# Attention and routed feed-forward block on one core: normalisation, transposition and router logits moved out of the front stage into the first units of the stream

## What is computed

```python
xn = _layernorm(x, axis=-1)
# attention: 16 heads of 64, causal
q, k, v = (einsum('btd,hdk->bhtk', xn, W) for W in (Wq, Wk, Wv))
wei = softmax(where(causal, q @ k.T * 64 ** -0.5, -inf))
attn = (wei @ v).reshape(...) @ Wo + bo
# feed-forward: a shared expert and the best 2 of 16 experts a token
router = sigmoid(xn @ gate_w + gate_b)           # 256 x 16
values, indices = top_k(router, 2); values = values / sum(values)
mlp = lambda x, wg, wu, wd: (silu(x @ wg) * (x @ wu)) @ wd
out = x + attn + xn + mlp(xn, shared) + sum(values * mlp(xn, experts[indices]))
```

## Time and profile before

| | us |
|---|---|
| median of 3 runs | 1964.02 (1962.02 to 1964.59) |
| the profiled execution | 1970.11 |
| its span in the trace | 1968.4 |
| front stage, to the stream's first transfer | 95.6 |
| unit 0 of the stream begins | 117.0 |
| the last `weigh` begins | 1956.3 |

### The profile page before, as it was taken

The page is one execution under the profiler, slowest core; times in us unless marked ns, Lnnn a source line. Parts: engine busy times, 40 slices in busy tenths (PEclk is TensorE's granted clock), DMA queues, the critical chain, the costliest instruction groups (busy, mean ns, idle before and its releaser), DMA issues.

```text
span 1968.4 us, 53517 instructions
## 1 busy us (share of the span) xinstructions
PE 1905.5 (97%) x20558; PEld 1751.7 (89%) x20558; DVE 1406.9 (71%) x4086; ACT 1208.4 (61%) x3340; POOL 1019.5 (52%) x1512
## 2 busy tenths in 40 slices
PE   6889999999999998999999999999999999999998
PEld 6878898988888898999998999999999989888897
DVE  7568886767676675666666667666667888888865
ACT  4356566666666665666665666666666666656564
POOL 2243447777777643344343343344444767687742
PEclk9999999999999999999999999999999999999999
DMA  9524422434343312545545445445422232323200
GB/s 260 187 106 176 161 77 85 143 110 136 109 145 109 126 51 83 181 162 163 166 148 170 155 152 168 161 161 183 146 92 76 87 119 87 117 89 119 76 23 12
DMA packets 158603, 249.92 MB, mean 127 GB/s; under 512 B 27280, under 2 KB 112528, under 8 KB 158352
## 3 DMA queue, kind: packets, MB, share of 16 engines
q1 hardware_dynamic: 134688, 150.79, 23.5%
q0 software_dynamic: 23664, 95.70, 15.0%
HBM read 151.54 MB, written 94.90 MB: 125 GB/s over the span
## 4 chain that ended last, share of the span: by engine, by line
PE 73%; POOL 12%; issue 7%; ACT 2%; DVE 1%; DMA 0%; POOLq 0%; SPq 0%; DVEq 0%
PE d_bank L658 15%; PE d_bank L710 11%; PE d_bank L696 10%; PE d_bank L685 9%; PE d_bank L671 7%; POOL d_probs L1305 7%; PE d_bank L726 7%; PE d_bank L784 6%; POOL queued_rows L1268 4%; PE d_bank L771 3%; PE d_bank L742 2%; ACT d_probs L853 2%; PE d_bank L794 1%; PE d_bank L731 1%; POOL d_base L1257 1%
## 5 line engine op out<-in xcount | busy, mean ns | idle before, releaser
L1305 POOL TENSOR_SCALAR d_probs<-d_probs,d_inverse 128x512 f32<-128x512 f32 (+3 forms) x1024 | 553.6, 556 | 767.4 <-DVE d_inverse L985 765.6
L853 ACT ACTIVATE d_probs<-d_probs,d_bias 128x512 f32<-128x512 f32 (+3 forms) x1024 | 561.1, 553 | 1.2 <-DVE d_bias L979 1.2
L979 DVE CUSTOM_DVE_ANT_0 d_probs<-d_bank,mask 128x512 f32<-128x512 f32 (+3 forms) x1024 | 438.9, 484 | 2.1 <-PE d_bank L696 1.9
L658 PE MATMUL d_bank<-d_xnt,wqk_all 128*128 128x512 f32 x1536 | 417.6, 408 | 1.5 <-DVE d_xnt L1032 1.5
L696 PE MATMUL d_bank<-d_ks,d_qs 64*128 64x512 f32 (+3 forms) x3072 | 317.4, 335 | 14.0 <-issue 12.0
L658 PEld LDWEIGHTS d_bank<-d_xnt,wqk_all 128*128 128x128 f32 x1536 | 276.6, 192 | 55.7 <-DVE d_xnt L1032 1.7
L846 ACT ACTIVATE d_probs_t<-d_bank 128x512 f32<-128x512 f32 (+1 forms) x384 | 188.8, 526 | 213.6 <-PE d_bank L685 213.5
L710 PE MATMUL d_bank<-d_probs_t,d_v 128*64 128x128 f32 x5120 | 308.6, 276 | 0.0
L710 PEld LDWEIGHTS d_bank<-d_probs_t,d_v 128*64 128x64 f32 x5120 | 277.7, 137 | 17.2 <-issue 5.4
L696 PEld LDWEIGHTS d_bank<-d_ks,d_qs 64*128 64x128 f32 x3072 | 252.0, 188 | 35.6 <-issue 19.4
L685 PEld LDWEIGHTS d_bank<-ident_r,d_probs_moved 64*128 64x128 f32 x5120 | 232.8, 136 | 38.6 <-issue 36.9
(11 more groups left out here) (122 smaller groups left out, 2296.9 us busy)
## 6 DMA issues: line engine op xcount, KB each, us to landing
queued_rows<-d_zeros SPq DMA_DIRECT2D x79, 256.0 KB, 2.4
d_x<-queued_rows SPq DMA_DIRECT2D x79, 256.0 KB, 3.4
routed_rows<-d_y SPq DMA_DIRECT2D x79, 256.0 KB, 2.3
expert_rows<-d_w SPq DMA_DIRECT2D x32, 384.0 KB, 3.8
a_x_in<-in_L_attn_x SPq DMA_DIRECT2D x16, 512.0 KB, 7.1
xn_rows<-a_xn SPq DMA_DIRECT2D x16, 512.0 KB, 5.2
d_normal<-xn_rows SPq DMA_DIRECT2D x32, 256.0 KB
d_base<-in_L_attn_x SPq DMA_DIRECT2D x32, 256.0 KB, 3.0
```

Source lines behind the costliest of these rows:

```text
L658: last = pe.matmul(to[:, :], wqk[:, n % PAIRS, "qk".index(kind), wa, k, :], xnt[n // PAIRS % 2][:, xb, k, :], start=first, stop=(k == KD - ...
L853: act.activation(part, part, ACT.Exp, bias=bias[:, i, h:h + 1], scale=-1.0, accum_out=total[which][:, at % 4:at % 4 + 1]).then_inc(exp_don ...
L979: dve.tensor_tensor_reduce(out=probs[:, i, h, 0:cols], in0=bank(f"s{fill}", u, h)[:, at * P:at * P + cols], in1=mask[:, T - cols:T], scale ...
L1305: pool.tensor_scalar(part, part, inverse[which][:, at % 4:at % 4 + 1], 1.0, ALU.mult, ALU.mult).then_inc(norm_done, 1)
```

## The change

The front stage keeps the loading and splitting of weights (now the gate weights too, HI and LO) and the row statistics: all means, variances and inverse deviations stay in SBUF (`mean_var`, `rstd`, 64 columns of rows each). It loads `x` for these alone; the rows of batches 0 to 2 stay in SBUF as `xa`. It has no normalisation, no transposition, no logits, no store of rows and no work of TensorE; there is one root for all batches, behind the last.

The rest moves into the stream at 17 places (`FRONT`): place 0 in step -3, then two a step from -2 to 5, at the two points of a unit at which the expert tiles have theirs later. At place n GpSimd normalises batch n + 1 (4 instructions of 128x256, in place in `xa`), TensorE forms the logits of batch n - 1 (24 products of 16 columns in float32r, three passes) and turns batch n (8 transposes), ScalarE and VectorE split it, and SyncE stores the rows of batch n (512 KB), the split operand of batch n - 1 (1024 KB, to `xnt_split`) and loads the rows of batch n + 2 (512 KB). Batches 1 to 15 of the split operand are loaded back (1024 KB each) two batches ahead of their use; the turns of u = 3, 11, ... go, and the projections wait for that load. The sigmoid follows in unit 6. Routing, clearing, scatter, expert tiles and gather all begin 7 units later: scatter in units 19 to 50, expert tiles in 56 to 96, gather in 98 to 125.

```diff
...
-FIRST_SCATTER = 12
+ROUTE_AT = 7
+FIRST_SCATTER = ROUTE_AT + 12
+KEPT = 3
...
-        DEEP = 4
+        DEEP = 6
...
-                def store(b):
-                    sp.wait_ge(xn_done, b + 1)
-                    sp.dma_start(dram["xn"][b], xn[b % DEEP][:, :, :]).then_inc(xn_stored[b % DEEP], DMA)
...
+                sp.dma_start(gate_in[:, :, :], ins["L0_ffn_gate_w"].rearrange("(k p) e -> p k e", p=P)
                              ).then_inc(const_loaded, DMA)
-                sp.dma_start(gate_w[:, :, :], ins["L0_ffn_gate_w"].rearrange("(k p) e -> p k e", p=P)
+                sp.dma_start(keep["gate_b"][:, :], ins["L0_ffn_gate_b"].rearrange("(a n) -> a n", a=1).broadcast_to([P, E])
                              ).then_inc(const_loaded, DMA)
-                for b in range(1, DEEP):
+                for b in range(B):
                     load_x(b)
-                for b in range(B):
-                    store(b)
...
-                act.wait_ge(lg_out, B)
-                act.activation(probs[:, :, :], probs[:, :, :], ACT.Sigmoid).then_inc(sig_done, 1)
+                act.wait_ge(const_loaded, 2 * DMA)
+                act.activation(gate_w[:, HI, :, :], gate_in[:, :, :], ACT.Copy).then_inc(gate_hi, 1)
+                for n in range(len(loads)):
+                    split(n)
+                act.wait_ge(stage_loaded[len(loads)], 3 * DMA)
+                act.activation(shared[:, HI, :], shared_in[:, :], ACT.Copy).then_inc(shared_hi, 1)
+                act.wait_ge(mean_done, B)
+                act.activation(std[:, :], mean_var[:, :, 1], ACT.Sqrt, bias=eps[:, 0:1]).then_inc(std_done, 1)
 
             @block.vector
...
                 for b in range(B):
-                    if b + 1 < B:
-                        moments(b + 1)
-                    normalise(b)
-                    if b >= 2:
-                        take_logits(b - 2)
-                for b in range(B - 2, B):
-                    take_logits(b)
...
+        FRONT = {place: n for n, place in enumerate([(-3, 1)] + [(u, part) for u in range(-2, B // 2 - 2) for part in range(2)])}
...
+        def front(u, part):
+            n = FRONT.get((u, part))
+            if n is None:
...
+            return {kind: n - back for kind, back in (("lg", 1), ("n0", 0), ("n1", 0)) if 0 <= n - back < B}
+
+        def turned(n):
+
+            return xnt[0] if n == 0 else ax if n % 2 else xnt[1]
...
+                def load_xa(b):
+                    sp.wait_ge(*xn_kept(b - KEPT))
+                    sp.wait_ge(n_ready, (b - KEPT + 1) * KD)
+                    for part in range(2):
+                        two = slice(part * 2, part * 2 + 2)
+                        sp.dma_start(xa[b % KEPT][:, two, :], x_src[b, :, two, :]).then_inc(xa_loaded[b % KEPT], DMA)
+
+                def store_xn(b):
+                    sp.wait_ge(x_normal, (b + 1) * QT)
+                    for part in range(2):
+                        two = slice(part * 2, part * 2 + 2)
+                        sp.dma_start(dram["xn"][b, :, two, :], xa[b % KEPT][:, two, :]).then_inc(xn_stored[b % KEPT], DMA)
+
...
+                def store_turned(b, hl):
+                    sp.wait_ge(n_out, (b + 1) * KD)
+                    for k in range(KD):
+                        sp.dma_start(turned_rows(b, hl, k), turned(b)[:, hl, k, :].bitcast(F32)).then_inc(ax_stored[b % 2], DMA)
+
+                def load_xnt(b, hl, k):
+                    if hl == 0 and k == 0:
+                        sp.wait_ge(ax_stored[b % 2], (b + 1) // 2 * KD * HALVES * DMA)
+                        if b == 1:
+                            sp.wait_ge(ax_stored[0], (B // 2 - 1) * KD * HALVES * DMA)
+                            sp.wait_ge(lg_ready, B - 1)
+                        else:
+                            sp.wait_ge(p_ready, 2 * PAIRS * (b - 1))
+                            sp.wait_ge(v_ready, PAIRS * (b - 1))
+                    sp.dma_start(xnt[b % 2][:, hl, k, :].bitcast(F32), turned_rows(b, hl, k)).then_inc(xnt_loaded[b % 2], DMA)
...
+                        n = FRONT.get((u, slot // 2))
+                        if n is not None:
+                            if slot % 2 == 0 and n < B:
+                                store_xn(n)
+                            if n >= 2:
+                                store_turned(n - 1, slot % 2)
+                            if slot % 2 and KEPT <= n + 2 < B:
+                                load_xa(n + 2)
+                        if u == -2 and slot == 1:
+                            for part in range(2):
+                                load_normal(0, part)
+                        if u == B // 2 - 3 and slot >= 2:
+                            for n in range(2):
+                                load_xnt(1, slot - 2, n)
+                        if k == PAIRS - 2 and 0 <= b and b + 2 < B:
+                            load_xnt(b + 2, slot // 2, slot % 2)
+                        for n in range((u - ROUTE_AT) * 8 + slot * 2, (u - ROUTE_AT) * 8 + slot * 2 + 2):
...
                 def project(kind, u):
                     to, n = take(kind, u), u + 2
-                    pe.wait_ge(n_out, (n // PAIRS + 1) * KD)
+                    if n < PAIRS:
+                        pe.wait_ge(n_out, KD)
+                    else:
+                        pe.wait_ge(xnt_loaded[n // PAIRS % 2], (n // PAIRS + 1) // 2 * KD * HALVES * DMA)
                     first = True
...
+                def turn(n):
+                    pe.wait_ge(x_normal, (n + 1) * QT)
                     for k in range(KD):
-                        to = take(f"n{k}", u)
+                        to = take(f"n{k}", n)
                         for q in range(QT):
-                            last = pe.transpose(to[:, q * P:(q + 1) * P].bitcast(F32R), normal[:, q, k * P:(k + 1) * P],
+                            last = pe.transpose(to[:, q * P:(q + 1) * P].bitcast(F32R), xa_r[n % KEPT][:, q, k * P:(k + 1) * P],
                                                 ident[:, :])
                         last.then_inc(n_ready, 1)
+
+                def logits(n):
+                    to = take("lg", n)
+                    pe.wait_ge(n_out, (n + 1) * KD)
+                    for q in range(QT):
+                        for k in range(KD):
+                            for xb, wa in PASSES:
+                                last = pe.matmul(to[:, q * P:q * P + E], turned(n)[:, xb, k, q * P:(q + 1) * P],
+                                                 gate_w[:, wa, k, :], start=(k == 0 and (xb, wa) == PASSES[0]),
+                                                 stop=(k == KD - 1 and (xb, wa) == PASSES[-1]))
+                    last.then_inc(lg_ready, 1)
 
                 def count(kind, u):
...
+                def split_normal(n):
                     for k in range(KD):
-                        act.wait_ge(n_ready, b * KD + k + 1)
-                        act.activation(xnt[b % 2][:, HI, k, :], bank(f"n{k}", u)[:, :], ACT.Copy).then_inc(n_hi, 1)
+                        act.wait_ge(n_ready, n * KD + k + 1)
+                        if n >= 3 and k == 0:
+                            act.wait_ge(ax_stored[n % 2], (n - 1) // 2 * KD * HALVES * DMA)
+                        act.activation(turned(n)[:, HI, k, :], bank(f"n{k}", n)[:, :], ACT.Copy).then_inc(n_hi, 1)
...
+                def take_logits(n):
+                    dve.wait_ge(lg_ready, n + 1)
+                    dve.tensor_tensor(gates[:, n * QT:(n + 1) * QT, :],
+                                      bank("lg", n)[:, :].rearrange("p (q n) -> p q n", q=QT)[:, :, 0:E],
+                                      keep["gate_b"][:, None, :].broadcast_to([P, QT, E]), ALU.add).then_inc(lg_out, 1)
...
+                def front_part(u, part):
+                    n = front(u, part)
+                    if "lg" in n:
+                        take_logits(n["lg"])
+                    if "n0" in n:
+                        split_normal(n["n0"])
...
+                    route(u - ROUTE_AT, 0)
+                    front_part(u, 0)
                     n = tick(u, 0)
...
+                def normalise_rows(n):
+                    if n >= KEPT:
+                        pool.wait_ge(xa_loaded[n % KEPT], n // KEPT * 2 * DMA)
+                    for q in range(QT):
+                        col = n * QT + q
+                        pool.tensor_scalar(xa[n % KEPT][:, q, :], xa[n % KEPT][:, q, :], keep["mean_var"][:, col, 0:1],
+                                           keep["rstd"][:, col:col + 1], ALU.subtract, ALU.mult).then_inc(x_normal, 1)
...
+                for n in range(2):
+                    normalise_rows(n)
...
+                    n = FRONT.get((u, 0))
+                    if n is not None and n + 1 < B:
+                        normalise_rows(n + 1)
...
+                    n = FRONT.get((u, 1))
+                    if n is not None and 0 < n and n + 1 < B:
+                        normalise_rows(n + 1)
...
```

218 lines of the change are left out of this document (82 added, 136 removed).

## The result

The changed kernel takes 2000.4 us (median of 4, 1994.4 to 2001.7) against 1964.3 for the kernel before (4, 1962.0 to 1964.7): ratio 1.0177, interval 1.0165 to 1.0189. It is slower by 36 us, where I forecast 8 us faster, and 24 us above the upper end of the range. The profiled execution took 2001.73 us, 31.6 more than that of before.

The account below looks back on a forecast made before the run. TensorE, busy 97% of the span, was taken to bound the stream, and loads the shortened front stage. Terms -46.5 + 9.3 + 13.0 + 14 + 2 = -8.2 gave 1961.9 us profiled, 1955.8 as forecast median, range 1938 to 1976.

Parts of the forecast that it names:

- stream's first transfer: End of the front stage: without turns and logits there, the stream begins at 49.1 us instead of 95.6, -46.5 us.
- from there to unit 0: Stream's start to unit 0: row normalisation, four logits groups and four turns make it 30.7 us against 21.4, +9.3.
- units 0 to 5: First six stream units: twelve logits groups +16.0, clock falls +14 and added turns 7.5, together +37.5 us.
- unit 6 to the end: Rest of the stream: fourteen turns gone, -10.5, and a costlier gather at the end, +2, together -8.5 us.
- twelve groups: Logits products added to TensorE in units 0 to 5, 1.33 us a group, 16.0 us together.
- the clock: Units 0 to 5: logits groups pull TensorE to its lower level at five of 12 places, +14 us, between 0 and 50.
- eleven turns: Transposes of batches moved into units 0 to 5, 0.75 us each, 8.2 us together.
- the end: Last units, where the later gather has three items instead of one: +2 us, between 0 and 6.
- The price of the logits: 24 passes of 16 columns on TensorE: 55 ns each at the upper level, 1.33 us a group; 2.7 at the lower.
- Rival (4): Weight loads set the logits' price, 99 ns a product, 1.05 us more for each of 15 groups: 1971.5 us, chance 0.08.
- Rival (2): Logits pull the clock down at most places, 34.8 us instead of 14: slower than before, 1976.6 us, chance 0.20.
- no transfer would pace the places: Stream places moving 2.1 MB: 7.6 us of transfers fit narrowly into 8.4 us of TensorE, so nothing was added.

Follow-up runs that it names:

- the cheap logits: Changed kernel with gate weights loaded and 512 token columns streamed, 6 products a group instead of 24: 1962.9 us; with rows also normalised on VectorE, 1951.0 us.

## Why the prediction was wrong

Against the profiled spans, 1968.4 and 2000.0:

| term | predicted | measured |
|---|---|---|
| stream's first transfer, 95.6 before | -46.5 | -43.1 (52.45) |
| from there to unit 0, 21.4 before | +9.3 | +20.8 (42.2) |
| units 0 to 5, 84.1 before (117.0 to 201.1) | +37.5 | +53.9 (138.0) |
| unit 6 to the end, 1767.3 before | -8.5 | 0.0 (1767.3) |
| sum | -8.2 | +31.6 |

The third term is the prediction's twelve groups, +16.0, the clock, +14, and eleven turns for one that goes, 8.2 - 0.7 = 7.5; the other fourteen turns, -10.5, and the end, +2, make the fourth. What was measured in the third: twelve groups at 2.68 us from start to start (116.02 to 118.75 and 126.39 to 129.02 with 128 columns), 32.2; the turns, about 7.3; falls of the clock, 24.5 (138.0 against 113.5 with 128 columns); and 9.0 less, which the kernel before lost there itself and which I hadn't booked (3.8 us of idle TensorE, and 10.3 us at half speed, of which half counts as lost). That is 55.0, for 53.9.

**The price of the logits was the step that failed.** I took 55 ns a product from half of the front's 221 ns and 1.33 us a group. It is 114 ns and 2.74 us (2.68 from start to start): 16 us more for the 12 groups of units 0 to 5, and about 7 more for the four ahead of unit 0 (2.6 for the first, at the lower level, and 3 x 1.4). The row 221 ns was of the lower level, and there a product of the changed kernel also takes 220 ns (5.29 us for 24): a plain float32 instruction of before cost as much as one float32r product, not two. The halving for the passes was the error; the halving for the clock was right.

The Trainium skill (TensorE: Matmul & The Clock Gate, LDWEIGHTS (loading the stationary operand)) puts a weight load at its columns divided by 1.2 in ns, 107 for 128 columns. These traces agree within a tenth at the upper level, 114 and 116 ns, and not at the lower one, 220 ns. I had set it aside because a turn's instruction takes 99 ns; that was the wrong row to weigh it by, and why a turn is cheaper stays open. Rival (4), at 99 ns, was the nearest to the price.

**The clock was the right mechanism at the wrong size.** I feared that a group may act like a wait and counted 5 stretches of 2.8 us. It did at nearly every place, 57.9 us at half speed, and it is worth 24.5 us in units 0 to 5, for the 14. Rival (2), falls at most places, thus came true, and rival (4) with it. I had treated them as alternatives, each with a chance of its own, though nothing in the profile made them so; no case of mine had both (the 15.7 of (4) on top of the 1976.6 of (2) would be 1992), and the result lies above every one. That the products' few columns are the cause is shown by the run with 128 columns; that a wait isn't needed is seen in unit 2. In the front stage the same sign had stood in the earlier trace rows: 15 us at 100% busy and still the lower level.

**The way to unit 0.** Besides the logits' 7 us, GpSimd's four row blocks took 4.8 us where I had 2.0, and TensorE waited 3.21 us ahead of the third turn. That is 13.0, for the 11.5 that were missing. I had priced the row blocks by the earlier trace rows, 486 ns, an operation of the same shape with one value a partition fewer; over all 64 by shape:

```profile
L1334 POOL TENSOR_SCALAR xa<-xa,mean_var,rstd 128x256 f32<-128x256 f32 x64 | 77.1, 1217 | 11.1 <-POOLq L131 11.1
```

1217 ns each. The wait was priced at nothing: I placed the end of this normalisation, which stands behind the base rows, before TensorE would ask. GpSimd stood 7.23 us for the reload of batch 0, began the rows at 72.5 and needed 4.8 us for four, while TensorE was ready at 74.2. At 486 ns each they would have been done at 74.5 (an estimate from these rows), so the reload used up the room and the price made the wait. "It has room", from the busy share of the whole span (52%), said nothing of this. Moved to VectorE a block takes 422 ns; that is worth 11.8 us with the cheap logits and 2.3 with those of the changed kernel.

**The front stage** came out nearly as forecast, 52.45 against 49.1, within the 56 that I had set. The term that was too small is VectorE, busy 9.79 of 10 us from 40 to 50: its statistics ran late and ended the stage, where I had let only the last batch's 1.8 us show. With the loads in another order GpSimd ends it at nearly the same time.

**Unit 6 to the end.** I had -8.5, measured are 0.0. The end takes 7.9 us more (from the `weigh` of unit 118 to that of 127, 1870.6 to 1987.2 = 116.5, against 108.6), where I had 2, between 0 and 6, and what follows it another 0.8. From the `weigh` of unit 6 to that of 118 it is 8.7 us shorter (1628.4 against 1637.0), for the turns' -10.5. The routing, now in these units, costs 1.0 more than what stood there (233 to 392 us: 3.5 idle and 3.4 at half speed; before, 201 to 360 us: 2.5 and 3.4), so the size looks right, but it isn't shown: the kernel with only the routing later, which keeps its turns, takes 1629.9 us there, and the profiled execution of before was itself 6 us above its median. That the end's loss goes with the shift is shown in kind: with nothing but the routing later it is 6.7 us. In all, the ten kernels with the shift take 111.5 to 116.9 us there, the two without it 107.5 and 108.6. Why it is 3 us in some and 8 in others stays open.

**Right** were the gain in front, that no transfer would pace the places of units 0 to 5, and that ScalarE's split doesn't wait for one. One sign failed without weight for the time: I had said that the first expert tile's wait for its rows must keep its length, and it went from 4.6 to 3.0 us. The view of waits by engine, of before and then of after:

```profile
PE d_bank L794 <- DMA d_x<-queued_rows: 4.6, 1, 4.6
```

```profile
PE d_bank L791 <- DMA d_x<-queued_rows: 3.0, 1, 3.0
```

## What to carry to other kernels

A float32r product with 128 loaded columns cost its weight load here, 114 to 116 ns, whether it streamed 16 columns or 128: load the narrow operand and stream the wide one, even if the result has to be turned back (2.0 instead of 2.74 us a group). Work that moves from a stage bound by transfers into one bound by TensorE is paid at TensorE's price there, with its effect on the clock, and what it cost at its old place tells that only if level and operation are the same. An engine's room is to be read in the stretch where the work lands, with what stands ahead of it in that engine's program, and the price of an operation from one with as many operands.

## What the runs showed of the hardware

- Products of 16 columns pull the granted clock from the upper (2.4 GHz) to the lower level (1.2 GHz) though TensorE is busy without a gap: 57.9 us at half speed with 16 columns, none with 128 columns in the same number of products, in the same order. More columns made the kernel 25 us faster.
- At the lower level the weight-load-bound product takes nearly twice as long, 220 ns instead of 114.
- GpSimd takes 1217 ns for (x - mean) * rstd on 128x256, with two operands of one value a partition. For a multiplication by one such value and by the constant 1.0 it takes 486 ns. VectorE takes 422 ns for the former.
- A front stage with logits of 512 columns runs at the upper level from 61 us on (turn 0.87 us for 8) where that with 16 columns ran at the lower to its end (1.23 us for 8).
